# Projections of three batches moved into the first stage, and the causal mask moved from TensorE to VectorE from batch 1 on

## The reference

```
xn = layernorm(x)                               # no scale, no shift
q  = xn @ Wq + bq + pe      (8 heads of 128)    # pe: sinusoidal positions, the same for every head
k, v = split(xn @ Wkv + bkv);  k = k + pe       # one key and one value head for all 8 query heads
s  = softmax(causal(q k^T / sqrt(128))) v, all heads side by side, @ Wo
g  = silu(mixture of experts(xn))               # 8 experts, 256 -> 1024 -> 256, relu, top 2 by a router
out = x + s * g
```

## Time and profile before

| | |
|---|---|
| median of 3 runs | 1077.34 us |
| span of the profiled execution, first to last instruction | 1078.8 us |
| busy: TensorE, VectorE, ScalarE, GpSimd | 990.9, 857.8, 641.9, 336.8 us |
| scores L1242; values L1265; output projection L1281 | 218.8; 189.7; 66.9 us on TensorE |
| row maxima L1426; low halves L1462 | 183.1; 199.4 us on VectorE |
| exponentials L1346; high halves L1376 | 187.0; 187.0 us on ScalarE |
| probabilities turned by DMA, in the chain that ended last | 5% of the span |

### The profile page before, as it was taken

How to read it: one execution, slowest core, us unless ns; L and a number is a source line. 1 busy time by engine, 2 the same in 40 slices (tenths; PEclk the granted TensorE clock), 3 DMA queues, 4 the chain that set the end, 5 groups by cost and what they waited for, 6 DMA issues and landing times.

```text
span 1078.8 us, 25081 instructions
## 1 busy us (share of the span) xinstructions
PE 990.9 (92%) x8686; PEld 778.5 (72%) x8686; DVE 857.8 (80%) x1535; ACT 641.9 (59%) x1358; POOL 336.8 (31%) x350
## 2 busy tenths in 40 slices
PE   0747999999999999998989889999999999999997
PEld 0536888888888898865656667767777677677776
DVE  6985776666766455569999999998999999999971
ACT  2722333233333333357888888878888878788860
POOL 3215999989995000020101002121212111112111
PEclk9968999999999999999999999999999999999999
DMA  8778666666666322149887879798999878888992
GB/s 273 211 287 182 157 181 177 174 179 184 171 172 147 95 60 65 46 121 159 171 154 141 157 142 186 152 164 150 172 189 178 150 150 162 153 171 160 181 179 95
DMA packets 410137, 172.58 MB, mean 160 GB/s; under 512 B 351994, under 2 KB 399940, under 8 KB 409252
## 3 DMA queue, kind: packets, MB, share of 16 engines
q1 hardware_dynamic: 352816, 129.80, 57.5%
q10 hardware_dynamic: 50724, 23.50, 8.6%
q0 software_dynamic: 6480, 17.70, 6.5%
HBM read 52.84 MB, written 31.72 MB: 78 GB/s over the span
## 4 chain that ended last, share of the span: by engine, by line
PE 37%; DVE 10%; DMA 5%; ACT 2%; issue 1%; SPq 0%; ACTq 0%; DVEq 0%
PE b_psO L1265 11%; PE b_psS L1242 11%; PE b_psJ L1281 5%; DMA b_pT<-b_ph 5%; PE b_psJ L1201 5%; DVE b_nmax L1426 3%; DVE b_ph L1462 3%; PE b_psS L1292 2%; PE b_psO L1267 1%; PE b_psS L1201 1%; DVE b_outs L1468 1%; ACT b_pr L1346 1%; ACT b_ph L1376 1%; PE b_psS L1245 1%; DVE b_Q L1449 1%
## 5 line engine op out<-in xcount | busy, mean ns | idle before, releaser
L933 PE MATMUL psU<-bxT,w_p 128*128 128x256 f16 (+1 forms) x1920 | 287.5, 262 | 13.3 <-DVE w_p L276 9.3
L1008 ACT ACTIVATE h<-psU,bias 128x256 f32<-128x256 f32 (+1 forms) x320 | 125.3, 448 | 273.6 <-PE psU L933 171.5
L942 PE MATMUL psY<-w_p,hp 128*128 x1704 | 273.4, 273 | 2.1 <-DVE hp L1034 2.1
L1242 PE MATMUL b_psS<-b_kp,b_Q 128*128 128x512 f16 (+3 forms) x1152 | 218.8, 326 | 1.5 <-PEq L1086 1.5
L1346 ACT ACTIVATE b_pr<-b_psS,b_nmax 128x1024 f32<-128x1024 f32 (+7 forms) x256 | 187.0, 735 | 47.9 <-DVE b_nmax L1426 27.1
L933 PEld LDWEIGHTS psU<-bxT,w_p 128*128 x1920 | 188.4, 98 | 34.0 <-issue 15.1
L1265 PE MATMUL b_psO<-b_pT,b_vp 128*128 128x256 f16 x1536 | 189.7, 274 | 20.3 <-issue 13.5
L1462 DVE SCALAR_TENSOR_TENSOR b_ph<-b_pr,b_rrec,b_ph 128x1024 f16<-128x1024 f32 (+7 forms) x256 | 199.4, 810 | 0.0
L1376 ACT ACTIVATE b_ph<-b_pr,b_rrec 128x1024 f16<-128x1024 f32 (+7 forms) x256 | 187.0, 768 | 15.4 <-DVE b_rrec L1455 14.1
L1032 DVE CAST hp<-h 128x512 f16<-128x512 f32 (+1 forms) x160 | 88.9, 556 | 133.7 <-ACT h L1008 127.5
L1426 DVE TENSOR_REDUCE b_nmax<-b_psS 128x1 f32<-128x1024 f32 (+7 forms) x256 | 183.1, 746 | 13.9 <-PE b_psS L1245 12.4
(11 more groups left out here) (187 smaller groups left out, 1027.1 us busy)
## 6 DMA issues: line engine op xcount, KB each, us to landing
wstage<-in_L_ffn_w SPq DMA_DIRECT2D x48, 256.0 KB
expert_rows<-rowx SPq DMA_DIRECT2D x67, 128.0 KB
expert_outputs<-y ACTq DMA_DIRECT2D x31, 256.0 KB
a_x_all<-in_L_attn_x SPq DMA_DIRECT2D x8, 512.0 KB, 9.7
a_w_raw<-in_L_ffn_w SPq DMA_DIRECT2D x4, 1024.0 KB, 9.4
xn_split<-a_xp SPq DMA_DIRECT2D x4, 1024.0 KB, 8.9
xn_turned<-a_xT SPq DMA_DIRECT2D x3, 1024.0 KB, 13.7
b_x_row<-in_L_attn_x SPq DMA_DIRECT2D x24, 128.0 KB, 2.5
```

Of the source, the lines that this page charges most:

```text
L933: mm = eng.matmul(psU[w % U][:, g % 2, 0:tiles * P].rearrange("p (t r) -> p t r", t=tiles), weight(n, a * W1 + c * H + g * P, P), bxT[n % ...
L942: mm = eng.matmul(psY[n % 2][:, t, :], hp[n % 2][:, a, g, t * P:(t + 1) * P], weight(n, 2 * W1 + (2 * g + b) * D, D), start=(g == 0 and k ...
L1008: a = eng.activation(h32[w % 4][:, g, 0:rows], psU[w % U][:, g, 0:rows], ACT.Relu, bias=bias[:, ds(e * HT + 2 * q + g, 1)], scale=1.0 / WS)
L1242: mm = eng.matmul(dst, Q[n % 3][:, a, u * P:(u + 1) * P], kb[:, c, lo:lo + w], start=(kk == 0), stop=(kk == 2 and not last))
```

## The change

Three things are done.

1. The first stage makes 24 projection jobs in place of 4: keys, all eight query heads and the values of batch 0, and the keys of batches 1 and 2. GpSimd now splits all of Wq in this stage (two pieces of 2 x 512 columns; before 2 x 128 there, the rest in the expert stage). ScalarE copies each job's sums to SBUF, and both ScalarE and TensorE wait for the 24 copies before the first expert block.
2. In the expert stage ScalarE's queue stores the 24 raw results (3 in each of blocks 0 to 7) and loads them again one by one (from block 3 on); in blocks 4 to 28 VectorE adds positions and makes the low half, ScalarE the high half, and both halves go to DRAM. In the attention stage SyncE's queue loads the halves of query heads 2 to 7 and of the keys of batches 1 and 2. Twenty jobs leave the attention stage's list: 18 of batch 0 and the two for the keys of batch 2. 
3. From head 8 on the mask's matmul is left out, and VectorE's row maximum becomes a `tensor_tensor_reduce` that adds a band (zeros, and the mask in its last 128 columns), negates, writes the result back to PSUM and reduces it by minimum. The exponential takes it with scale -1.

```
+EARLY = [("K", 0), ("Q", 0), ("V", 0)] + [("Q", h) for h in range(1, HEADS)] + [("K", 1), ("K", 2)]
+EARLY_JOBS = [(kind, m, j) for kind, m in EARLY for j in range(2)]
...
-            if job:
+            if job and job not in EARLY_JOBS:
...                                              # routing, TensorE
+            if e in (3, 4):
+                project(e - 3)
...
-        for r in range(3):
-            project(r)
+        for q in range(2, 6):
+            project(q)
         eng.wait_ge(s_bz, 3)
         counts()
-        project(3)
+        for q in range(6, 11):
+            project(q)
         for s in range(CHUNKS):
             place(s)
-        eng.wait_ge(s_kc, 4)
+            if s < 5:
+                project(11 + s)
+        for q in range(JOBS_UP, NJ):
+            project(q)
+        eng.wait_ge(kqc_, NJ)
...                                              # routing, GpSimd
-        for i, (full, p) in enumerate(((wkv_f, wkv_p), (wq_f, wq_p))):
+        for i, (full, p) in enumerate(((wkv_f, wkv_p), (wq_f[:, :, 0:512], wq_h[:, :, :, 0:512]),
+                                       (wq_f[:, :, 512:], wq_h[:, :, :, 512:]))):
...                                              # experts, ScalarE, behind the relus of block n
+            if 0 <= r < NJ:
+                high(r)
+            if 1 <= r <= NJ:
+                put_halves(r - 1)
+            if -1 <= r < NJ - 1:
+                load_raw(r + 1)
+            for i in range(PUT * n, min(PUT * n + PUT, NJ)):
+                put_raw(i)
...                                              # attention, TensorE
-                        last = lo + w == w_all
+                        last = lo + w == w_all and n < BANDED
...                                              # attention, ScalarE
-                                       bias=nmax[:, at:at + 1], accum_out=rsum[:, at:at + 1])
+                                       bias=nmax[:, at:at + 1], scale=1.0 if k < 5 * BANDED else -1.0, accum_out=rsum[:, at:at + 1])
...                                              # attention, VectorE
+                    if k < 5 * BANDED:
+                        a = eng.tensor_reduce(nmax[:, at:at + 1], s, AX.X, ALU.max, negate=True)
+                    else:
+                        a = eng.tensor_tensor_reduce(s, s, band[:, T - w:T], -1.0, LARGEST, ALU.add, ALU.min, nmax[:, at:at + 1])
...                                              # attention, SyncE
+                if i == 1 and 1 <= n < HEADS - 2:
+                    early_in(("Q", n + 2), Q[(n + 2) % 3], ql[(n + 2) % 3])
```

## The result

The changed kernel takes 1153.7 us (median of 5 runs) against 1077.4 for the one before (5 runs): a ratio of 1.071, 95% interval 1.067 to 1.075. The forecast was 1074 with a range to 1092, so it was wrong in sign and by far in size. The profiled executions have spans of 1160.7 and 1078.8 us, 81.9 apart. That is 5.6 more than the 76.3 us between the medians: the profiled execution of the changed kernel was the slowest of its five (1162.6 us), so a few us of what follows are that execution's own.

What follows compares the result with a forecast made beforehand. Bounds: a chain of small steps before 85 us, TensorE in the expert stage, VectorE in batch 0, then TensorE with VectorE right behind. 5.0 + 0 - 13.0 + 4.4 = -3.6 us, hence 1074 us, range 1059 to 1092.

Steps and rivals of the forecast that it cites:

- Expert stage: Expert stage: added rounds and transfers are covered by TensorE; taken as 0, bounds -1 and +5 us.
- First stage: Before the expert matmuls: four terms and a credit, a loss of +5.0 us, bounds -1.5 and +23.
- Term 1: First stage: GpSimd's longer split of Wq slows VectorE to about 0.6 of its pace; +5 us, bounds 0 and +15.
- Term 3: Behind `place`: eight jobs, the last copy and the load of the expert's number exceed the idle time; +2.6 us.
- Term 2: `place` in the first stage: five jobs between its eight parts, +5.5 us at the lower clock or nothing; +1.5 taken.
- Term 4: First 54 expert matmuls: their slowness goes with matmuls right before them; -1.7 us.
- terms 4 and 5: Term 5, expert stage's start-up: TensorE's idle wait for gathered rows absorbs most of its later start; -2.4 us.
- Batch 0: Attention of batch 0: 18 jobs leave, 0.72 us each; -13 us, bounds -23 and -7.
- Rival E: Batch 0 becomes bound by DMA and half of its gain is gone; 1080 us, chance 0.16.
- Batches 1 to 3: Attention, batches 1 to 3: the mask's move costs VectorE 0.64 us a head; a loss of +4.4 us together.
- rival B: Batches 1 to 3: the second instruction hides in VectorE's 0.67 us to spare; 1061 us, chance 0.17.
- Rival D: First stage: VectorE stands still for all of GpSimd's extra 15 us; +15 in place of +5, 1084 us, chance 0.08.

Runs made afterwards that it cites:

- e1: Changed kernel with positions moved behind VectorE's first split, low half behind its third, high half behind ScalarE's second relu pair; 1101.7 us, 1.018 of the kernel before.
- e7: e1 without the stores of raw projections and all but two of their loads; 1090.2 us (one run), expert stage 386.8.
- e9: e1 with GpSimd splitting only the 128 columns of head 0 of Wq, used by every Q projection; 1093.4 us (one run).
- e3: Changed kernel with the mask added by TensorE in all 32 heads as before; 1155.7 us, 1.069 of the kernel before.
- e5: e1 without the loads of Q halves in batch 0 from head 3 on; 1100.2 us (one run), batch 0 132.8.
- e6: e1 with 12 projections that nobody reads added on TensorE in heads 0 to 5 of batch 0; 1100.3 us (one run), batch 0 129.4.

## Why the prediction was wrong, step by step

- **Expert stage, "taken as 0, bounds -1 and +5": +71.0.** This step lost the forecast. It compared busy time with room (VectorE 242 of 386 us) and said that the waits added are for transfers issued a block earlier. One of them is not: ScalarE's high half waits for VectorE's positions of the same block. The prediction saw what is queued behind the stores in ScalarE's queue (the rows' load) but not the next block's relus, on which VectorE and then TensorE wait. Cost 52.4 us (e1), 17 of it by slower matmuls (busy 400.1 us against 382.8). For the transfers it worked out a DMA share of 0.7, a mean; the stores are bunched in the first eight blocks, where the share is 0.98, and with the loads they cost 18.2 us in e1 against e7, 9 to 16 in the other kernels.
- **First stage, +5.0: +15.4.** Term 1, VectorE beside GpSimd, +5, came out at 6.2 (e9), and that is luck: two errors cancel. GpSimd was done at 41.4, not 48.6, only 7.8 us later than before and not 15; and beside it VectorE did not run at 0.6 of its pace but stood still for whole instructions, about 0.36 of its pace between 31.3 and 41.8 us. Term 3: jobs behind the placing cost 2.9 us (12.2 us from the places known to the first expert matmul, 9.3 before), as the 2.6 said; the last copy and the load of the expert's number, put there at 1.6 without a row, took 1.9 (98.63 to 100.52). Term 2, +1.5, is the one that failed in size: with the 6.2 us taken off, the placing still ends 6.3 us later. Jobs in front of the counts give 1.3 of it, and 2.35 us per part with a job, at the higher clock, the most of the rest. The step "nothing if the extra work keeps it at the higher one" was bad arithmetic: 1.04 + 1.31 = 2.35 is over 1.45, and these are the times at the higher clock. Term 4: 54 matmuls in 6.08 us, not 7.55, so 1.5 of the 1.7; terms 4 and 5 fall in the stage behind, whose 386.8 us in e7 shows nothing of them.
- **Batch 0, -13: -0.7, and -3.7 to -4.0 in e1 to e3.** VectorE was rightly named as the leader, and the work did leave it (130.7 to 110.9 us busy). What took its place is a loop through the transpose, with TensorE's clock in it. None of the rivals had the clock. Rival E had the place (heads 1 to 5, the queue with the probabilities) but the wrong cause for most of it: at most 2.3 us by the added loads (e5), 5.7 by the clock (e6), each from one profile. With the clock held, 129.4, the term would have been -9.7.
- **Batches 1 to 3, +4.4: -3.9.** Its price of 0.08 us per maximum is 0.02: five groups of a head start to start take 5.50 us with the new pairs and 5.32 with reductions, so 0.18 per head, not 0.64. That is rival B's mechanism, a second instruction that does not show in the time. The Trainium skill's rule of two instructions (VectorE: DVE Perf Modes, section Two Vector instructions with no wait between them) agrees with the rows, which do show two; their second one costs next to nothing in time. The keys' jobs taken from heads 12 and 13, -2.4 in the prediction, gave -3.0 with the mask left on TensorE (18.8 and 19.0 us before, 17.4 each in e3), and that is most of the gain of this stage. What is left is within what kernels with the same work differ by here: the seven with the mask on VectorE and without these jobs took 391.3 to 394.4 us for heads 9 to 31.
- **Rival D** missed in time and had the mechanism. The sentence that two subtractions "went through" beside GpSimd misread its row: the second of them waited for GpSimd's instruction to end. VectorE stood still for most of the 7.8 us that GpSimd now works longer and lost 6.2; D's +15 took GpSimd's time too long, as term 1 did. The Trainium skill (SBUF — State Buffer, section SBUF: two separate sides) puts it as an exclusive lock held for an instruction, behind which the other engine fully blocks. This trace agrees: the subtraction that started behind GpSimd's 2.64 us took 2.60 us in place of 0.68.

No version of the change measured here beats the kernel before. The best of those that compute what the reference does, e6, has 1100.3 us against 1079.6: the first stage's +13 to +15 us and the transfers' 9 to 18 us stand against at most 10 us to win in batch 0. Not measured: shortened jobs in the first stage, a smaller set of early jobs, more filler, and filler in the kernel before, in front of the first expert matmul.

## What to carry to other kernels

Before calling work hidden because an engine has idle time, write down for each added wait what stands behind it in that engine's order, and follow it until it either reaches the instruction that was waited for (a loop, with a period that can be added up) or an engine with slack; mean busy shares say nothing about it. Look first at where the kernel before has the same wait: its four rounds had the positions behind the first split, and moving them behind the third made the loop. Place such a wait behind work that the other engine finishes early in the block, and spread transfers over a stage instead of bunching them. When TensorE is relieved next to a wait of some us, price the matmuls behind that wait at the lower clock.

## What the runs showed of the hardware that was not expected

- VectorE stood still behind GpSimd's instructions: of VectorE's subtractions and normalisations those that started beside one ended 0.14 to 0.55 us after it, one of them after 2.60 us in place of 0.68.
- Useless matmuls shortened a stage: 12 projections more, 5.7 us less, with the granted clock at 0.98 and not 0.91.
- VectorE's read of its accumulator after a custom maximum shows as 0.14 us, and its follower starts 0.00 us after the read's own start; with it a maximum takes 0.01 to 0.03 us more than the plain reduction, from start to start.
- GpSimd's split of 1024 columns of Wq took 5.3 us (30.79 to 36.06), 5.1 ns a column, where the 768 columns before took 8.4 ns each on average.
